# Seventy unread products of the identity ahead of TensorE's work, in a one-core patch-embedding, attention and feed-forward layer

## What is computed

```python
h = layernorm(img2patches(x), g1, b1)              # over 768 features
h = layernorm(h @ W + b, g2, b2)                   # 768 -> 192
z = plain_layernorm(h)
q, k, v = split(z @ in_proj_weight.T + in_proj_bias)       # 12 heads of 16
attn = softmax(normalize(q) @ normalize(k).T * exp(min(logit_scale, LIMIT)))
h = h + (attn @ v * head_scale) @ out_w.T + out_b          # attention over the 32 images
z = plain_layernorm(h)
up, gate = split(bitlinear(z, w_in, g_in))         # quantized rows, ternary weights
h = h + bitlinear(silu(gate) * up, w_out, g_out)
```

## Time and profile before

| | |
|---|---|
| median of three runs | 140.13 us (139.06 to 142.69) |
| the profiled execution | 140.62 us |
| its span, first to last instruction | 138.7 us |
| mean granted TensorE clock over the span | 0.918 of full speed |
| busy: PE, PEld, DVE, ACT, POOL | 105.4, 82.0, 108.2, 81.6, 66.0 us |

### The profile page before, as it was taken

How to read it: one execution, slowest core, us unless ns; L and a number is a source line. 1 busy time by engine, 2 the same in 40 slices (tenths; PEclk the granted TensorE clock), 3 DMA queues, 4 the chain that set the end, 5 groups by cost and what they waited for, 6 DMA issues and landing times.

```text
span 138.7 us, 4589 instructions
## 1 busy us (share of the span) xinstructions
PE 105.4 (76%) x1784; PEld 82.0 (59%) x1784; DVE 108.2 (78%) x388; ACT 81.6 (59%) x168; POOL 66.0 (48%) x160
## 2 busy tenths in 40 slices
PE   0003999999989999999997954989799877655610
PEld 0003999888778798986866642657676644234400
DVE  4059028999999999999999998959999999695210
ACT  0305246998987669523836582065589789786400
POOL 7003001565329621486136866614874798787000
PEclk9999999999999999999999997579999997797555
DMA  4999999996000000000000000000000010000110
GB/s 99 225 243 263 176 171 264 156 175 132 2 0 0 5 2 5 5 2 5 5 0 5 0 5 0 5 2 5 5 5 10 23 33 28 21 26 13 42 44 29
DMA packets 24093, 7.75 MB, mean 56 GB/s; under 512 B 20038, under 2 KB 23495, under 8 KB 24072
## 3 DMA queue, kind: packets, MB, share of 16 engines
q1 hardware_dynamic: 20310, 6.43, 24.4%
q10 hardware_dynamic: 3762, 1.03, 3.9%
HBM read 6.58 MB, written 0.88 MB: 54 GB/s over the span
## 4 chain that ended last, share of the span: by engine, by line
PE 30%; DVE 30%; ACT 13%; POOL 9%; issue 8%; DMA 4%; ACTq 2%; DVEq 0%
PE bank L612 5%; PE bank L594 4%; PE bank L613 4%; DMA xs<-in_x_dram 4%; PE bank L624 4%; POOL yw L337 3%; PE bank L585 3%; PE bank L529 2%; DVE pT L878 2%; DVE bst L764 2%; DVE mx L869 2%; ACTq L232 2%; PE bank L686 2%; ACT xp L441 2%; DVE ax L933 1%
## 5 line engine op out<-in xcount | busy, mean ns | idle before, releaser
L594 PE MATMUL bank<-w_emb_g,xT 128*128 128x192 f32 x108 | 19.6, 331 | 0.0
L585 PE MATMUL bank<-ident,xp 128*128 128x128 f32 x54 | 8.2, 292 | 12.6 <-ACT xp L441 12.6
L594 PEld LDWEIGHTS bank<-w_emb_g,xT 128*128 128x128 f32 x108 | 17.4, 190 | 0.6 <-ACT xT L448 0.2
L612 PE MATMUL bank<-w_qkv,xhT 97*128 97x384 f32 (+1 forms) x36 | 13.4, 455 | 2.2 <-DVE on L886 1.8
L299 POOL TENSOR_TENSOR rs<-mv,mhalf 128x1 f32<-128x1 f32 x9 | 5.3, 589 | 19.6 <-DVE mv L786 19.6
L585 PEld LDWEIGHTS bank<-ident,xp 128*128 128x128 f32 x54 | 6.6, 150 | 13.1 <-issue 12.6
L764 DVE BATCH_NORM_STATS2 bst<-xs 128x6 f32<-128x384 f32 x18 | 8.8, 538 | 6.1 <-DMA xs<-in_x_dram 6.1
L337 POOL TENSOR_TENSOR yw<-yy,gout_bc 128x512 f32<-128x512 f32 x9 | 11.4, 1267 | 4.0 <-DVE yy L929 3.8
L613 PE MATMUL bank<-w_qkv,xhT 96*128 96x384 f32 (+1 forms) x36 | 12.7, 437 | 0.0
L669 PE MATMUL bank<-wi_t,xqT 96*128 96x512 bf16 x36 | 10.2, 409 | 1.4 <-ACT xqT L488 1.2
L441 ACT ACTIVATE xp<-xs,mv 128x768 f32<-128x768 f32 x9 | 8.3, 929 | 4.8 <-DVE mv L770 4.6
(11 more groups left out here) (135 smaller groups left out, 304.4 us busy)
## 6 DMA issues: line engine op xcount, KB each, us to landing
xs<-in_x_dram SPq DMA_DIRECT2D x30, 96.0 KB, 3.6
out_dram<-h_all SPq DMA_DIRECT2D x18, 48.0 KB
wi_raw<-in_L_ffn_w_in_dram SPq DMA_DIRECT2D x1, 768.0 KB, 7.3
xs<-in_x_dram ACTq DMA_DIRECT2D x6, 96.0 KB, 4.0
w_emb_sb<-in_L_tok_W_dram SPq DMA_DIRECT2D x1, 576.0 KB, 7.0
w_qkv_raw<-attn_in_proj_weight_dram ACTq DMA_DIRECT2D x1, 432.0 KB
wo_raw<-in_L_ffn_w_out_dram SPq DMA_DIRECT2D x1, 384.0 KB, 8.5
gout_bc<-in_L_ffn_g_out_dram SPq DMA_DIRECT2D x1, 256.0 KB, 4.0
```

The source lines that it names most:

```text
L585: mm = nc.tensor.transpose(dst, xp[:, t % 3, P * k:P * (k + 1)], ident[:, :])
L594: mm = nc.tensor.matmul(emb_bank, xT[:, t % 3, P * k:P * (k + 1)], w_emb_g[:, 3 * (k % 2) + k // 2, :], start=(k == 0), stop=(k == KF - 1))
L612: nc.tensor.matmul(dst, xhT[:, t % 3, 0, :], w_qkv[:, 0, cols], start=True, stop=False)
```

## The change

A step `warm` is added to TensorE's stream. `warm(0)` waits for the identity and issues 58 products of the identity by its own first 64 columns, all into the first 64 columns of bank 0; `warm(1)` waits for the first statistics of tile 0 and issues 12 more. Both stand ahead of `xT_(0)`, which writes bank 0 anew; nothing reads what they wrote. All else keeps its order. The line numbers of TensorE's functions from `bmm` on, and of VectorE's, become larger by nine.

```diff
         @block.tensor
         def _(pe):
 
+            def warm(part):
+
+                if part == 0:
+                    pe.wait_ge(c_id, 1)
+                else:
+                    pe.wait_ge(bst1_ok, 1)
+                for _ in range((58, 12)[part]):
+                    nc.tensor.matmul(xT_lo[:, 0:64], ident[:, :], ident[:, 0:64], start=True, stop=True)
+
...
-            xT_(0); bmm(); xT_(1, (xT_ok, 2)); emb(0, (p_bias, 1)); qkvT(); xT_(2, (xT_ok, 4)); emb(1, (h0s_ok, 1))
+            warm(0); warm(1); xT_(0); bmm(); xT_(1, (xT_ok, 2)); emb(0, (p_bias, 1)); qkvT(); xT_(2, (xT_ok, 4))
```

More of the change, by code:

```diff
@@ L687, in ff2 @@
                 mm.then_inc(o2_ps, 1)
-            xT_(0); bmm(); xT_(1, (xT_ok, 2)); emb(0, (p_bias, 1)); qkvT(); xT_(2, (xT_ok, 4)); emb(1, (h0s_ok, 1))
-            xT_(3, (xT_ok, 6)); emb(2, (h0s_ok, 2)); xT_(4, (xT_ok, 8)); emb(3, (h0s_ok, 3)); woTp((p_qkvE, 3))
-            xhT_(0, (xT_ok, 10)); wsum(); qkv(0); xhT_(1); emb(4, (h0s_ok, 4)); xT_(5, (xhT_ok, 2)); woT()
-            qkv(1, (qk_ok, 1), (vx_ok, 1)); emb(5, (h0s_ok, 5)); xhT_(2); qkv(2, (qk_ok, 2), (vx_ok, 2)); xhT_(3)
+            warm(0); warm(1); xT_(0); bmm(); xT_(1, (xT_ok, 2)); emb(0, (p_bias, 1)); qkvT(); xT_(2, (xT_ok, 4))
+            emb(1, (h0s_ok, 1)); xT_(3, (xT_ok, 6)); emb(2, (h0s_ok, 2)); xT_(4, (xT_ok, 8)); emb(3, (h0s_ok, 3))
+            woTp((p_qkvE, 3)); xhT_(0, (xT_ok, 10)); wsum(); qkv(0); xhT_(1); emb(4, (h0s_ok, 4)); xT_(5, (xhT_ok, 2))
+            woT(); qkv(1, (qk_ok, 1), (vx_ok, 1)); emb(5, (h0s_ok, 5)); xhT_(2); qkv(2, (qk_ok, 2), (vx_ok, 2)); xhT_(3)
             wiT((p_woE, 1), (p_mean, 2)); xT_(6, (xhT_ok, 4)); sc(0, (p_oE, 1)); qkv(3, (qk_ok, 3), (vx_ok, 3))
```

## The result

The changed kernel has a median of 157.75 us over four runs (157.17 to 161.07), against 139.59 (138.53 to 142.69) for the kernel before on the same chip: a ratio of 1.1315, with a 95% interval of 1.1196 to 1.1434. The profiled execution took 157.43 us with a span of 155.6, 16.9 us more than the 138.7 of before. I had forecast 144.5. The time is that of the first rival, in which the clock stays at half; I had given it 0.22 and 159.3 us.

What follows compares the result with a forecast made beforehand. The pipeline's start was taken to bound the kernel; a 4.4 us delay of `xT_(1)` added to the profiled 140.6 gave 145.0, or 144.5 us for the median, range 142.2 to 160.0.

Steps and rivals of the forecast that it cites:

- first rival: TensorE's new products don't lift the half clock: PE free at 31.9, `xT_(1)` 19.2 us late, 159.3 us; chance 0.22.
- The start is what bounds: When the pipeline gets going matters, not PE or DVE alone; from 17.44 us on the program is a rigid pattern.
- If `xT_(1)` starts later or earlier by d, everything behind it does: Behind the second set of transposes, at 17.44 us, any shift d passes through; no long wait there is for a DMA.
- Each new product is two records with a load each: In `warm` on PE, 70 float32 products make 140 loads of 128 columns and 140 products of 64.
- The load decides what a record costs, and it doubles at the half clock: For the 140 new records on PE: 0.110 us each at the full clock, 0.217 at the half clock.
- The rival in which repeated loads cost nothing: Reloading the identity in `warm` is free, so `xT_(1)` starts at 16.0, 1.46 us early, 138.7 us; chance 0.10.
- the one with a load that ignores the clock: All 140 records of `warm` take 0.110 us in either state; delay 2.2 us, 142.3 us; chance 0.08.
- If the clock rises 4.4 us after that, as it did after 12.65, then 4.4 / 0.217 = 20 records run slow: In `warm`, from about 1.5 us: 20 records slow, the other 120 take 13.2 us, PE through at 19.1 us.
- my sum: At the start: PE through at 19.1, `xT_(1)` at 21.8 instead of 17.44, 4.4 us late; 144.5 us median.
- the rival of the half clock: The first rival: all 140 records of `warm` slow, PE free at 31.9, `xT_(1)` at 36.7, 159.3 us; chance 0.22.
- the engine as a whole never pauses: Argument against the rival of the half clock, for the new products on PE; that rival got 0.22.
- The 280 more instructions also change when PE's instructions are fetched; I cost that at nothing: In PE's instruction stream, the effect of the added instructions on fetching was taken as nothing, within the scatter.

Runs made afterwards that it cites:

- mixb: The program of mix timed again: median 141.5 us over six scattered runs, against 140.44 for the kernel before; no interval.
- mix: Against the changed kernel: 16 products of 128 columns, then 22 of 64, and 2 more behind the first statistics, instead of 70; one run, 138.44 us.
- c128: Against the changed kernel: the 70 new products stream all 128 columns of the identity instead of 64; one run, 148.67 us.
- c128b: The program of c128 run again: median 143.5 us over four runs, ratio 1.0223 to the kernel before.
- l64: Against the changed kernel: the 70 products load only 64 columns of the identity and write 64 partitions; median 138.26 us, ratio 0.9809 to the kernel before.
- tr70: Against the changed kernel: the 70 new products become 128-column transposes of the identity; median 145.3 us of ten scattered runs, ratio 1.0156 to the kernel before.
- pad100: Against the changed kernel: 25 products of 32 x 16 (100 instructions) replace the 70, none behind the statistics; 142.74 us against 140.44 before, ratio 1.0133.

## Why the prediction was wrong, point by point

- The start is what bounds, and a delay of `xT_(1)` goes through rigidly: right. 17.95 us at the start became 16.9 in the span, and the missing 1.1 us is mostly the gap that went away. "If `xT_(1)` starts later or earlier by d, everything behind it does" is wrong for "earlier": in mixb 1.55 us of lead ended in the wait for pixels at 21 us. The earlier trace rows has no wait for a DMA because at that start the pixels had landed in time.
- Each new product is two records with a load each: right, x140.
- The load decides what a record costs, and it doubles at the half clock: right. I took 0.217 and 0.110 us; measured were 0.214 (the change) and 0.112 (mix, whose 64-column records stand that far apart). The rival in which repeated loads cost nothing is refuted, and so is the one with a load that ignores the clock (333 ns in the change, 192 in c128 at the full clock).
- "If the clock rises 4.4 us after that, as it did after 12.65, then 4.4 / 0.217 = 20 records run slow": this is the step that failed. The 4.4 us came from a stretch of transposes and 192-column products (first product at 12.65 us, first clock record at 17.0), and I carried it over to a stretch that alternates loading and streaming. It never rose there; all 140 ran slow, 0.214 us each. The price of that is 120 x (0.214 - 0.110) = 12.5 us, which takes my 144.5 to 157.0, beside the measured 157.75. That they lie so close is in part luck: slower first transposes and `bmm` (3.96 us for my 2.74) and the 1.1 us given back later nearly cancel.
- Where the products do stream, my sum holds: in c128 PE was free at 18.95 (forecast 19.1), the second set of transposes started at 21.56 (21.8), and c128b had a median of 143.5 (144.5).
- In the rival of the half clock the terms were near: PE free at 31.4 (31.9), second set at 35.4 (36.7), because the clock rose earlier within `bmm` than I had it. That I gave it 0.22 rested on "the engine as a whole never pauses". The trace of before had no stretch bound by loads at the half clock, so nothing there decided it; I should have given both cases like chances, and named the one with the large price more plainly.
- "The 280 more instructions also change when PE's instructions are fetched; I cost that at nothing": wrong in kind. For this kernel it was a gain of some 0.8 us near 87 us, by luck of where the borders fell; with 100 instructions it is a loss of 2 us.

## What to carry to other kernels

In these runs the clock came up in the stretches whose products had as many columns as their loads (c128 at 5.1 us, l64 at 5.0, tr70 at 4.6), and not in 30 us of products with half as many: look at the load's own columns first, and check in the trace that the records become shorter. Work put ahead of a waiting engine has to be through when the data comes; count its records at the slow clock, since that is what one gets if the clock doesn't rise (140 x 0.213 = 30 us against 11 us of room). And when instructions are added to an engine with a dense stream, compare the idle stretches without a cause before and after, and the waits that last longer than what they are put down to, because a shift alone moved this kernel by 1.3% (pad100). A gain at the start held here only as far as the loads kept up with it (mixb: 1.55 us of lead, then 1.82 us of waiting for pixels).

## What the runs showed that I had not expected

- An unbroken stretch of 30 us, with products and loads side by side, left TensorE at the half clock (0.213 us a record); under 5 us of the same records it stayed at the full clock once it was there (mix, 0.112 us a record). Where between these two forms and c128's the limit lies wasn't tried.
- The clock rose with transposes of 128 columns alone on PE (tr70: at 4.6 us, 426 ns before and 272 behind it).
- After PE's wait of 2.8 us ahead of `qkv`, near 90 us, the clock was back within 4 us in c128b but only after over 20 us in c128, the same program; it went with a time 5 us longer.
- PE stops for 0.7 to 1.85 us at places a multiple of 256 of its trace's events apart, never less than 1.22 us after a 16 KB packet of instructions has come in, and 25 tiny products that nobody reads (pad100) made the kernel 1.3% slower by moving them.
